# A mask copied into the scores' banks by ScalarE, and two small products moved to other PSUM banks

## The reference

```python
for i in range(DEPTH):      # 6
    x = attn_layer(shift_tokens(x), Wqkv[i], q_scale[i], k_scale[i], Wo[i]) + x
    x = ffn_layer(shift_tokens(x), ln_g[i], ln_b[i], W1[i], b1[i], W2[i], b2[i]) + x
# attention, 16 heads of 64, windows of 32 positions that also see the window before:
mask = (it < jb) | (it > jb + w) | (jb == -1)
sim  = einsum('bhwie,bhwje->bhwij', bq, bk2) * 8.0     # q and k l2-normalised and rotated
attn = softmax(where(mask, -finfo.max, sim))
out  = einsum('bhwij,bhwje->bhwie', attn, bv2)
```

## Time and profile before

| | us |
|---|---|
| median of three runs | 3610.65 |
| lowest and highest | 3610.15 and 3612.87 |
| the profiled execution | 3610.44 |
| its span in the profile | 3608.3 |
| TensorE busy | 3439.6 (95%) |
| VectorE busy | 2965.6 (82%) |
| GpSimd busy | 2260.2 (63%) |
| ScalarE busy | 2116.0 (59%) |
| mean granted TensorE clock | 0.992 of full speed |

### The profile page before, as it was taken

The page is one execution under the profiler, slowest core; times in us unless marked ns, Lnnn a source line. Parts: engine busy times, 40 slices in busy tenths (PEclk is TensorE's granted clock), DMA queues, the critical chain, the costliest instruction groups (busy, mean ns, idle before and its releaser), DMA issues. The chain is left out here.

```text
span 3608.3 us, 101728 instructions
## 1 busy us (share of the span) xinstructions
PE 3439.6 (95%) x42643; PEld 2181.2 (60%) x42643; DVE 2965.6 (82%) x5526; ACT 2116.0 (59%) x4015; POOL 2260.2 (63%) x1361
## 2 busy tenths in 40 slices
PE   8999699999999999999999999999999999999996
PEld 4555366666666666666666666666666666666664
DVE  3444499898888999889889898899898998999983
ACT  2222256666666666666666666666666666666663
POOL 0000267777676777777777767677677776776763
PEclk9999799999999999999999999999999999999999
DMA  2000000100000100001000001000001000000000
GB/s 69 1 1 1 4 11 11 31 11 11 11 12 13 34 11 11 8 17 34 11 8 11 10 17 33 9 11 11 11 13 34 11 11 8 11 16 16 11 11 13
DMA packets 62284, 52.55 MB, mean 15 GB/s; under 512 B 11526, under 2 KB 59396, under 8 KB 61828
## 3 DMA queue, kind: packets, MB, share of 16 engines
q1 hardware_dynamic: 61828, 46.05, 4.8%
HBM read 43.93 MB, written 2.10 MB: 13 GB/s over the span
## 5 line engine op out<-in xcount | busy, mean ns | idle before, releaser
L416 POOL TENSOR_TENSOR cosp<-cosp,rr 128x1024 f32<-128x1024 f32 x384 | 722.7, 1903 | 694.8 <-DVE rr L65 694.8
L426 POOL TENSOR_TENSOR cosp<-cosp,sinp 128x1024 f32<-128x1024 f32 x384 | 903.2, 2369 | 56.7 <-DVE sinp L869 56.0
L607 PEld LDWEIGHTS ps<-px,w_vo 128*128 128x128 f32 x6144 | 705.5, 192 | 167.6 <-issue 88.8
L512 PE MATMUL ps<-w_qk,xs 128*128 128x512 f32 x1536 | 761.1, 618 | 35.9 <-ACT sq L719 30.3
L607 PE MATMUL ps<-px,w_vo 128*128 128x128 f32 x6144 | 727.7, 277 | 37.4 <-issue 32.9
L719 ACT ACTIVATE sq<-ps 128x1024 f32<-128x1024 f32 x384 | 392.0, 1021 | 462.7 <-DVE sinp L869 462.7
L866 DVE TENSOR_TENSOR cosp<-ps,tab 128x1024 f32<-128x1024 f32 x384 | 469.3, 1222 | 139.1 <-PE ps L512 138.3
L766 ACT COPY px<-ps 128x512 f32<-128x512 f32 x768 | 398.2, 598 | 283.7 <-PE ps L667 281.4
L875 DVE TENSOR_REDUCE ss<-sq 128x16 f32<-128x1024 f32 x384 | 455.1, 1185 | 94.8 <-ACT sq L719 94.8
L512 PEld LDWEIGHTS ps<-w_qk,xs 128*128 128x128 f32 x1536 | 262.7, 191 | 398.9 <-issue 397.2
L667 PE MATMUL ps<-pT,xtm 32*128 32x512 f32 x3072 | 459.0, 616 | 8.8 <-DVE pT L933 4.7
(11 more groups left out here) (102 smaller groups left out, 4419.3 us busy)
## 6 DMA issues: line engine op xcount, KB each, us to landing
tab<-in_tab SPq DMA_DIRECT2D x96, 128.0 KB, 2.0
qks<-in_scales SPq DMA_DIRECT2D x96, 128.0 KB, 3.3
w_qk<-in_L_ffn_Wqkv SPq DMA_DIRECT2D x12, 512.0 KB, 7.2
w_v<-in_wv_t SPq DMA_DIRECT2D x6, 512.0 KB, 8.8
w_o<-in_L_ffn_Wo SPq DMA_DIRECT2D x6, 512.0 KB, 9.7
x<-in_L_attn_x SPq DMA_DIRECT2D x16, 128.0 KB, 3.5
out<-w_v SPq DMA_DIRECT2D x16, 128.0 KB, 2.4
w<-in_L_ffn_W SPq DMA_DIRECT2D x6, 341.0 KB
```

What stands on the lines that cost most here:

```text
L416: eng.tensor_tensor(v, v, rr[:, B % 2, HEADS * i:HEADS * i + HEADS].unsqueeze(2).to_broadcast([P, HEADS, DH]), ALU.mult).then_inc(rot_read ...
L426: eng.tensor_tensor(cosp[:, A % 2, i, :], cosp[:, A % 2, i, :], sinp[:, i, :], ALU.add).then_inc(rot_added, 1)
L512: t = eng.matmul(ps[:, u, :], xs[:, n % ROUND, :], w_qk[:, n // TILES % 2, i, 512 * u:512 * u + 512], start=True, stop=True)
L607: t = eng.matmul(S0, w_vo[:, i // HP, i % HP, :], px[:, i, :], start=i == 0, stop=i == HEADS - 1)
```

## The change

Three things. `Y`, the output projection, now goes into a part of `G(3)`, and `X`, the transposed tokens, into a part of `G(0)`, both of them banks of k transposed; so TensorE no longer waits for `centered` ahead of them. The mask comes no longer from TensorE, but for the first tile: ScalarE copies it from SBUF (bf16, the same 64 columns for each of the 16 heads) into `S` as 128x1024 float32, behind its copy of the transposed tokens and ahead of `w_vo` or of transposed q, once `centered` of the tile before is there. TensorE waits for this copy (`mask_written`) ahead of the scores, and these accumulate on it. And since `Y` and `X` lie in banks that other products use, two waits move forward on TensorE: for `y_added` (VectorE has read `Y`) and `xt_evac` (ScalarE has read `X`), now ahead of the transposes of k in each step and, once a layer, ahead of the `w_vo` products.

```diff
--- before.py
+++ after.py
@@ -179,9 +179,9 @@
         ps = ctx.enter_context(nc.psum_tensor("ps", [P, 8, 512], F32))
         R = ps[:, 0:2, :]
         S = ps[:, 2:4, :].rearrange("p a (h k) -> p (a h) k", k=DH)
-        S0 = ps[:, 2, 0:P]
-        S1 = ps[:, 3, 0:P]
         G = lambda k: ps[:, 4 + k, :]
+        Y = G(3)[:, 0:P]
+        X = G(0)[:, 0:P]
 
         consts_in = sem("consts_in")
         abc_in = sem("abc_in")
@@ -223,6 +223,7 @@
         rot_ready = sem("rot_ready")
         turned = sem("turned")
         turn_evac = sem("turn_evac")
+        mask_written = sem("mask_written")
         sims_done = sem("sims_done")
         max_done = sem("max_done")
         centered = sem("centered")
@@ -596,23 +597,23 @@
                     after(eng, k_roped, 2 * A)
                     after(eng, sq_done, 2 * A)
                     project(A, 0)
-                if tile(C):
-                    eng.wait_ge(centered, C + 1)
                 if tile(E):
                     eng.wait_ge(px_evac, 4 * (E + 1))
                     if E % TILES == 0:
                         eng.wait_ge(vo_evac, 4 * (E // TILES + 1))
                     after(eng, y_added, E)
                     for i in range(HEADS):
-                        t = eng.matmul(S0, w_vo[:, i // HP, i % HP, :], px[:, i, :], start=i == 0, stop=i == HEADS - 1)
+                        t = eng.matmul(Y, w_vo[:, i // HP, i % HP, :], px[:, i, :], start=i == 0, stop=i == HEADS - 1)
                     t.then_inc(y_done, 1)
                 if tile(C):
                     after(eng, xt_evac, C)
-                    eng.transpose(S1, xs[:, C % ROUND, :], ident[:, :]).then_inc(xt_done, 1)
+                    eng.transpose(X, xs[:, C % ROUND, :], ident[:, :]).then_inc(xt_done, 1)
                 L = layer_of(s)
                 if L is not None:
                     eng.wait_ge(wv_in, 16 * (L + 1))
                     eng.wait_ge(wo_in, 16 * (L + 1))
+                    after(eng, y_added, E + 1)
+                    eng.wait_ge(xt_evac, C + 1)
                     for i in range(HP):
                         for x in range(2):
                             t = eng.matmul(G(2 * x + i // 4)[:, D * (i % 4):D * (i % 4) + D], w_v[64 * x:64 * x + 64, i, :],
@@ -628,6 +629,10 @@
                     eng.wait_ge(q_roped, 2 * A + 2)
                     eng.wait_ge(sq_done, 2 * A + 1)
                     project(A, 1)
+                if tile(E):
+                    eng.wait_ge(y_added, E + 1)
+                if tile(C):
+                    eng.wait_ge(xt_evac, C + 1)
                 if tile(B):
                     eng.wait_ge(rot_ready, 2 * B + 2)
                     turn(B, 1, K_BANKS)
@@ -638,13 +643,11 @@
                         eng.wait_ge(turn_evac, 4 * B + 3)
                     result(c)
                 if tile(B):
-                    if tile(E):
-                        eng.wait_ge(y_added, E + 1)
-                    after(eng, xt_evac, B)
-                    w = window(B)
-                    for h2 in range(2):
-                        eng.matmul(ps[:, 2 + h2, :].rearrange("p (h k) -> p h k", k=DH), ident_bf[:, :],
-                                   mask[:, DH * w:DH * w + DH].unsqueeze(1).to_broadcast([P, HP, DH]), start=True, stop=False, skip_group_check=True)
+                    if B == 0:
+                        for h2 in range(2):
+                            eng.matmul(ps[:, 2 + h2, :].rearrange("p (h k) -> p h k", k=DH), ident_bf[:, :],
+                                       mask[:, 0:DH].unsqueeze(1).to_broadcast([P, HP, DH]), start=True, stop=False, skip_group_check=True)
+                    after(eng, mask_written, B)
                     eng.wait_ge(turn_evac, 4 * B + 4)
                     for hp in range(HP):
                         for h2 in range(2):
@@ -654,7 +657,6 @@
                                                kT[rows, B % NG, hp, b, :], start=False, stop=hp == HP - 1, skip_group_check=True)
                     t.then_inc(sims_done, 1)
                 if tile(C):
-                    eng.wait_ge(xt_evac, C + 1)
                     eng.wait_ge(p_turned, C + 1)
                     if not tile(B):
                         for k in range(4):
@@ -774,7 +776,11 @@
                     square(A, 0)
                 if tile(C):
                     eng.wait_ge(xt_done, C + 1)
-                    eng.copy(xtm[:, C % NG, C % ROUND // 2, :], S1).then_inc(xt_evac, 1)
+                    eng.copy(xtm[:, C % NG, C % ROUND // 2, :], X).then_inc(xt_evac, 1)
+                if tile(B) and B:
+                    w = window(B)
+                    eng.wait_ge(centered, B)
+                    eng.copy(S, mask[:, DH * w:DH * w + DH].unsqueeze(1).to_broadcast([P, HEADS, DH])).then_inc(mask_written, 1)
                 L = layer_of(s)
                 if L is not None:
                     for k in (0, 2, 1, 3):
@@ -923,7 +929,7 @@
                     square_sum(A, 0)
                 if tile(E):
                     eng.wait_ge(y_done, E + 1)
-                    eng.tensor_tensor(xb[:, batches(E), tile_cols(E)], S0.rearrange("p (b t) -> p b t", b=GB),
+                    eng.tensor_tensor(xb[:, batches(E), tile_cols(E)], Y.rearrange("p (b t) -> p b t", b=GB),
                                       xa[:, batches(E), tile_cols(E)], ALU.add).then_inc(y_added, 1)
                 if tile(A):
                     rope(A, 1)
```

## The result

The changed kernel takes 3631.87 us, the median of its runs, against 3610.65 us before: a ratio of 1.0058, 95% interval 1.0046 to 1.0069. That is 21 us, where 6 were forecast, and 0.9 us above the upper end of the range. One of its five executions took 6382 us and is left out of the ratio; no trace of it is kept, so its cause stays open, and the median of the other four is 3630.86 us, 0.1 us inside the range.

A forecast was written before the change was run, and what follows sets the result against it. The prediction took VectorE's ring through k's projection, not TensorE, as the bound; 3610.44 - 6.2 (fourth steps) + 10.5 (layers' begins) + 2 (layer 0) + 0.5 (ends) gave 3617.2, forecast 3617 us, range 3605 to 3631.

The forecast's parts named there:

- VectorE's ring: Attention stage: rotation of q, square, projection of k, rotation of k, VectorE's remaining queue, next q; claimed to set the pace.
- Rival A: Whole kernel: TensorE sets the pace, so losing the mask products gives 3524 us, or 3574; chance 0.09.
- some 100 us less of TensorE's busy time: Sign that the main forecast is right: TensorE's busy time falls so, with more idle ahead of k's projection.
- late fourth steps: Fourth steps of turns: without the third step's mask products, VectorE waits 0.15 us less in 41 steps, gaining 6.2 us.
- The `centered` wait: Ahead of the output projection: already over before the last copy of `px`, so its removal was taken at nothing.
- ScalarE's copy: Ahead of transposed q and k on ScalarE: 1.02 us per copy, hidden under a 1.44 us wait, leaving 0.42 us.
- rival C: ScalarE's mask copy is dearer than its cover, from 1.44 us on; at 1.54 some 9 us, 3626; chance 0.04.
- The waits ahead of the transposes of k: Each step: a weight load is held about 0.1 us but done in time; taken at nothing, upper bound 14 us.
- Rival B: First transpose of k: the weight load's hold comes through, up to 0.1 us in 135 steps, 3631 us; chance 0.13.
- The layers' begins: Ahead of the `w_vo` products: the wait for `y_added` delays VectorE 2.1 us, five times, costing 10.5 us.
- Layer 0: Begin of the first layer: products wait for `xt_evac` at a low clock, costing 1.1 to 3.2 us, taken as 2.
- the ends: First and last tiles: some waits of the last three steps move half a us each way; taken at +0.5 us.

The follow-up runs named there:

- e3_moves_only: The changed kernel with the mask again made by TensorE's two products in each step and ScalarE's copy gone; Y, X and their moved waits kept: 3631.55 us.
- e6_null_products: The changed kernel with two products of an identity with zeros on TensorE where the mask's stood, ScalarE still copying the mask: 3630.54 us.
- e4_no_copy: The changed kernel without ScalarE's mask copy; from the second tile on nobody writes the mask, and TensorE waits for `centered`: 3631.54 us.
- e7_double_copy: The changed kernel with ScalarE's mask copy made twice in each step: 3651.84 us.
- e1_warm: The changed kernel with eight unread products on TensorE ahead of the two waits at the begin of layers 1 to 5: 3620.17 us.
- e5_less_dma: The changed kernel with 84 of the 96 loads of scale rows left out: 3632.08 us.
- e10_third_steps: The kernel before, with the change made only in the third step of each turn from step 9 on, 46 steps: 3605.86 us.

## Why the prediction was wrong, point by point

- *What bounds the kernel.* Right. VectorE's ring sets the pace; e3_moves_only and e6_null_products give TensorE its 0.52 us a step back and take no longer. Rival A is out. One sign named for my case, some 100 us less of TensorE's busy time, did not come (38 us); VectorE's waits are what bore the ring out.
- *The mask leaves TensorE.* The 6.2 us of late fourth steps were measured as 5.4, in 37 places for 41, from 0.66 to 0.51 us. What I took as nothing is a stall inside the scores that now start sooner: 3.8 us at 500 us and 1.8 us in eleven other places. The net gain is near nought.
- *The `centered` wait.* Nothing, as forecast, but its reason was read from too few steps. Before, half of the output projections did have a weight load that waited for `centered`:

```profile
PEld ps L607 <- DVE sh L950: 72.5, 96, 1.4
```

That none of this reached VectorE is shown by e3_moves_only, where the wait is gone from ahead of the projection and the fourth steps gain 0.02 us each.

- *ScalarE's copy.* 1.03 us for a taken 1.02, its cover 0.49 left for a reckoned 0.42, cost nought (e4_no_copy); rival C's price beyond the cover is real (e7_double_copy), but the copy doesn't reach it. The Trainium skill (ScalarE: Activation LUTs, step by step through the stages) calls ScalarE's way to PSUM the faster one. This copy into PSUM takes 1.03 us and the square, which writes SBUF, 1.02; no gain is seen, though the two also read from different places.
- *The waits ahead of the transposes of k.* The weight load was held, and nothing came of it: VectorE's wait for the square of k is 89.3 us for 89.2. Rival B is out.
- *The layers' begins.* This is the step that failed. The mechanism was right, and its size was right for what it priced: L619 starts right behind the add, 2.1 us late, five times 2.09 in e1_warm. The forecast stopped there. It carried the durations of the earlier trace rows over to a TensorE that had just stood 2.7 us idle. Instead the clock fell within the 32 products, which took 2.81 to 3.48 us for 2.06, and in four begins it stayed down over the transposes and most of k's projection: 4.84, 4.84, 3.60, 4.84 and 4.84 us, 23.0 in place of 10.5. The forecast had a clock of 0.55 behind 5.68 us of idle in hand and used it for layer 0 only, and a clock at full speed behind 1.29 us. Nearer rows stood in the last steps of the same trace, unread. Output projections, and the granted clock within each:

```profile
3547.62 3.81 PE L607 MATMUL ps<-px,w_vo 128*128 128x128 f32 x32 [2.23 <-issue]
...
3559.72 5.47 PE L607 MATMUL ps<-px,w_vo 128*128 128x128 f32 x32 [2.15 <-ACT px L766]
```

```profile
3547.62:3551.43 3.81, 3.81 (x34) 3.81 (x35) 1.47 (x2) 0.85 (x1) 1.34 (x1) 1.00 0.00 0
3559.72:3561.00 1.28, 1.28 (x6) 1.28 (x7) 0.00 (x0) 0.00 (x0) 0.00 (x0) 0.51 0.00 0
```

Behind 2.2 us of idle the clock either stays or falls. So each begin should have been priced at both levels, and the range should have held both.

- *Layer 0.* +0.3 us for 2 taken, below the range's 1.1: the products ran at the low clock, but transposes and projection behind them at the high one, and the products themselves were done in 3.4 us.

With 23.0 for 10.5, 0.3 for 2, 5.4 for 6.2, -2.5 for the ends' +0.5 and 5.6 for the stalls, the forecast's sum becomes 3631.4. That the upper end of the range, 3631, lies so near is luck: it was set by rival B, which did not happen.

## What to carry to other kernels

A wait on an engine that does not set the pace is priced by who waits at its end, and that pricing held to 0.01 us. But on TensorE a new wait has a second price: ask how long TensorE stands idle there, find the nearest rows of idle and granted clock, the start and end of the kernel included, and price all that follows at both levels up to the next waiting engine. Idle of the same length can go either way. Where the wait can't be avoided, a few products that nobody reads ahead of it may be cheaper than the clock; and where a change gains in only one of four kinds of steps, make it there and not in the steps in which it costs.

## What I had not expected of the hardware

- TensorE's granted clock fell behind idle times of only 2.2 to 2.7 us in kernels in which TensorE is 93 to 95% busy: at all five begins after, and in the six kernels with the moved wait and no work in the gap at 26 of 30. The other four are three of e7_double_copy (2.68 us idle) and one of e5_less_dma (2.45). At 1.29 us and 0.6 to 0.8 us (e1_warm) it stayed at 1.00. After, it fell within the first 2 us of the products and stayed low over the transposes and most of a projection, in one of five begins for less. The Trainium skill (TensorE: Matmul & The Clock Gate, part 1 on the clock gate) says that the clock is halved after idling and comes back after sustained work. The rows show both levels, 0.50 and 1.00; the four begins without a fall show that idling of this length does not always do it.
- TensorE can stand up to 2.3 us (2.55 in e4_no_copy) inside a run of 128 small products with no wait to show. With two products of 512 columns ahead of the scores in every step this is rare (0.8 us before, 0.2 in e6_null_products, none in e3_moves_only), without them in some or all steps it is not (10.8 to 28.2 us), and in e10_third_steps it comes in the steps that have them. Leaving out 84 of the 96 loads of scale rows made no difference (16.5 us for 14.9).
- Such a stall can pull the clock down too. After, 500 to 506 us:

```profile
500.00:506.00 6.00, 6.00 (x25) 2.29 (x22) 4.63 (x14) 1.91 (x4) 0.59 (x2) 0.50 0.07 18
```
